# One kernel of a two-layer graph network: who makes two high parts, which bank one aggregate takes, and when its product follows

## The reference

```python
h = relu(layernorm(x))
x = x + L0(h, adj)          # two graph convolutions, then LSTMs over windows
h = relu(layernorm(x))
x = x + L1(h, adj)          # normalised adjacency, W1, batch norm, relu, W2, batch norm

def L0(x, adj):
    h = relu(adj @ (x @ Wg0 + bg0))
    h = relu(adj @ (h @ Wg1 + bg1))
    for p in 1, 2, 3, 4:    # windows of p tokens, an LSTM of p steps over each
        last = lstm_last(Wih[p-1], Whh[p-1], windows(h, p))
        h[:, p-1::p] = last # the last token of each window is replaced
    return h

def L1(f, A):
    A_norm = A + I
    A_hat = A_norm * dinv[:, None] * dinv[None, :]
    hid = relu(batchnorm((A_hat @ f) @ W1.T + b1))   # over batch and nodes
    return batchnorm(hid @ W2.T + b2)
```

## Time and profile before

| what | value |
|---|---|
| median of three runs | 531.46 us (528.65 to 533.92) |
| profiled execution, its own time | 531.53 us |
| its span in the trace | 529.6 us |
| PE busy | 506.1 us, 96% |
| DVE busy | 415.2 us, 78% |
| ACT busy | 345.1 us, 65% |
| POOL busy | 198.3 us, 37% |

### The profile page before, as it was taken

The page is one execution under the profiler, slowest core; times in us unless marked ns, Lnnn a source line. Parts: engine busy times, 40 slices in busy tenths (PEclk is TensorE's granted clock), DMA queues, the critical chain, the costliest instruction groups (busy, mean ns, idle before and its releaser), DMA issues.

```text
span 529.6 us, 8039 instructions
## 1 busy us (share of the span) xinstructions
PE 506.1 (96%) x2720; PEld 431.9 (82%) x2720; DVE 415.2 (78%) x954; ACT 345.1 (65%) x670; POOL 198.3 (37%) x307
## 2 busy tenths in 40 slices
PE   7999997999999999999999999999899999999994
PEld 5788776989987789999887899998678998875574
DVE  4688788878868888786689887875977887976875
ACT  3546866656777676675686675767657686448744
POOL 6403045131401854343007741511533423337940
PEclk9999999999999999999999999999989999999998
DMA  7403000000011112020210201012604000600008
GB/s 241 119 20 101 0 1 20 22 0 22 2 58 41 42 58 81 1 80 1 80 61 20 80 20 42 1 60 101 218 22 139 21 2 20 239 0 1 0 19 300
DMA packets 17597, 31.21 MB, mean 59 GB/s; under 512 B 1514, under 2 KB 6292, under 8 KB 17428
## 3 DMA queue, kind: packets, MB, share of 16 engines
q1 hardware_dynamic: 16564, 30.17, 16.8%
q10 hardware_dynamic: 992, 0.52, 0.4%
HBM read 19.16 MB, written 11.53 MB: 58 GB/s over the span
## 4 chain that ended last, share of the span: by engine, by line
PE 52%; issue 19%; DVE 10%; POOL 7%; ACT 6%; POOLq 3%; DVEq 1%; DMA 1%; ACTq 0%
PE gate_ps L1273 10%; PE gate_ps L1269 10%; PE gate_ps L1270 10%; PE pre_ps L1269 4%; PE pre_ps L1273 4%; PE pre_ps L1270 4%; POOL x_pre L447 3%; PE post_ps L1269 2%; POOLq L445 2%; PE post_ps L1270 2%; PE post_ps L1273 2%; DVE cell L1077 2%; ACT gate L764 2%; DVE cell L1102 1%; PE pre_ps L1337 1%
## 5 line engine op out<-in xcount | busy, mean ns | idle before, releaser
L764 ACT ACTIVATE gate<-gate_ps,gate_bias 128x256 f32<-128x256 f32 (+2 forms) x312 | 164.0, 563 | 41.3 <-PE gate_ps L1273 39.8
L1273 PE MATMUL gate_ps<-by_class_lo,wih_hi 128*128 128x256 f32 (+2 forms) x264 | 84.9, 322 | 4.2 <-POOL by_class_lo L477 4.2
L1269 PE MATMUL gate_ps<-by_class_hi,wih_hi 128*128 128x256 f32 (+2 forms) x264 | 85.4, 324 | 1.2 <-DVE by_class_hi L1058 1.0
L1270 PE MATMUL gate_ps<-by_class_hi,wih_lo 128*128 128x256 f32 (+2 forms) x264 | 84.2, 319 | 0.0
L774 ACT ACTIVATE gate<-cell 128x512 f32<-128x512 f32 (+2 forms) x88 | 45.4, 516 | 45.2 <-DVE cell L1077 24.3
L477 POOL TENSOR_TENSOR by_class_lo<-h,by_class_hi 128x256 fp32r<-128x256 f32 (+1 forms) x40 | 34.3, 858 | 82.1 <-ACT by_class_hi L772 82.1
L1273 PE MATMUL gate_ps<-hstep_lo,whh_hi 128*128 128x256 f32 (+2 forms) x192 | 61.5, 320 | 0.0
L1269 PE MATMUL gate_ps<-hstep_hi,whh_hi 128*128 128x256 f32 (+2 forms) x192 | 61.2, 319 | 0.2 <-DVE hstep_hi L1096 0.2
L1270 PE MATMUL gate_ps<-hstep_hi,whh_lo 128*128 128x256 f32 (+2 forms) x192 | 60.6, 315 | 0.0
L1273 PEld LDWEIGHTS gate_ps<-by_class_lo,wih_hi 128*128 128x128 f32 x264 | 50.3, 191 | 8.1 <-POOL by_class_lo L477 4.9
L1269 PEld LDWEIGHTS gate_ps<-by_class_hi,wih_hi 128*128 128x128 f32 x264 | 50.5, 191 | 6.0 <-DVE by_class_hi L1058 1.6
(11 more groups left out here) (320 smaller groups left out, 1295.0 us busy)
## 6 DMA issues: line engine op xcount, KB each, us to landing
x_pre<-in_x SPq DMA_DIRECT2D x16, 256.0 KB, 2.7
x<-in_x SPq DMA_DIRECT2D x16, 256.0 KB, 2.7
z_spill<-z_ring SPq DMA_DIRECT2D x8, 512.0 KB, 2.9
z_back<-z_spill SPq DMA_DIRECT2D x8, 512.0 KB, 5.6
x_spill<-x SPq DMA_DIRECT2D x12, 256.0 KB, 2.0
x_back<-x_spill SPq DMA_DIRECT2D x1, 3072.0 KB, 11.5
out<-x_back SPq DMA_DIRECT2D x11, 256.0 KB, 2.5
x<-in_adj SPq DMA_DIRECT2D x1, 1024.0 KB, 6.2
```

The lines of the kernel that those rows point to most:

```text
L764: nc.scalar.activation(gate[:, tile_of(g), gt, 0:size], gate_ps[k % GATE_BANKS][:, 0:size], ACT.Tanh if gt == G_GATE else ACT.Sigmoid, bia ...
L1269: nc.tensor.matmul(ps, w[0], m[0], start=start, stop=False)
L1270: nc.tensor.matmul(ps, w[1], m[0], start=False, stop=False)
L1273: return nc.tensor.matmul(ps, w[0], m[1], start=False, stop=stop)
```

## The change

Turns 68 and 69 are now in a list `ACT_HI`. For them ACT makes the high part, in the turn that follows, behind that turn's first gate and after h is done; DVE makes the low part at the start of its next turn. The transposes of batch 11 stand behind turn 70 instead of 69, into `post_ps` instead of `pre_ps`, and its `turned` is done within turn 71. Batch 7's aggregate takes `pre_ps` instead of `post_ps`, waits for `turned(9)` instead of `turned(10)`, and stands ahead of the transposes behind turn 70. Its first W1 half moves from behind turn 71 to behind turn 72, where the second stands. The two banks change places for every later aggregate and half up to batch 10.

```diff
+ACT_HI = [g for g in range(N_TURNS) if TURNS[g][0] == ROUNDS - 1 and TURNS[g][2] == 1 and TURNS[g][1] == CHAINS - 1]
...
-LAST_POS = {"agg": {CARRIED: 4, CARRIED + 1: 7, CARRIED + 2: 10, CARRIED + 3: 14},
-            "hid0": {CARRIED: 5, CARRIED + 1: 8, CARRIED + 2: 11, CARRIED + 3: 16},
+LAST_POS = {"turn": {BATCHES - PER_ROUND - 1: 4}, "agg": {CARRIED: 4, CARRIED + 1: 7, CARRIED + 2: 10, CARRIED + 3: 14},
+            "hid0": {CARRIED: 6, CARRIED + 1: 8, CARRIED + 2: 11, CARRIED + 3: 16},
...
-IN_NEXT_TURN = range(LAST_TURNED, LATE - 1)
+IN_NEXT_TURN = range(LAST_TURNED, LATE)
...
             unit = 3 * (n - CARRIED) + ("agg", "hid0", "hid1").index(kind)
-            return pre_ps if unit > 0 and unit % 2 else post_ps
+            return pre_ps if unit >= 0 and unit % 2 == 0 else post_ps
 
         def turn_ps(n):
 
-            return pre_ps if n >= LAST_TURNED and n % 2 else post_ps
+            return pre_ps if n == LAST_TURNED + 1 else post_ps
...
+                    if j == 0 and g - 1 in ACT_HI:
+                        q = TURNS[g - 1]
+                        act.wait_ge(h_done, g)
+                        hi = by_class[0][:, q[1], :].rearrange("h (t b) -> h t b", b=SUBS)[:, :, q[4]]
+                        nc.scalar.activation(hi, cell[:, tile_of(g - 1), :], ACT.Copy).then_inc(class_hi, 1)
...
+                if g - 1 in ACT_HI:
+                    q = TURNS[g - 1]
+                    hi, lo = (part[:, q[1], :].rearrange("h (t b) -> h t b", b=SUBS)[:, :, q[4]] for part in by_class)
+                    dve.wait_ge(class_hi, CLASS_AT[q[0], q[1], 1, q[4]])
+                    low(lo, cell[:, tile_of(g - 1), :], hi).then_inc(class_lo, 1)
                 if step > 0:
...
-                    nc.vector.tensor_copy(hi, c_).then_inc(class_hi, 1)
-                    if g not in POOL_LO:
+                    if g not in ACT_HI:
+                        nc.vector.tensor_copy(hi, c_).then_inc(class_hi, 1)
+                    if g not in POOL_LO and g not in ACT_HI:
...
+                if ("agg", CARRIED) in POST_AFTER[slot]:
+                    pe.wait_ge(x1_ready, LATE - 2)
+                    agg_mms(CARRIED, post_bank("agg", CARRIED), 1)
                 for kind, n in POST_AFTER[slot]:
...
+                        elif n == LATE - 1:
+                            pe.wait_ge(x1_ready, n)
...
-                    if kind == "agg":
-                        if n == CARRIED:
-                            pe.wait_ge(x1_ready, LATE - 1)
-                        elif n > CARRIED:
+                    if kind == "agg" and n != CARRIED:
+                        if n > CARRIED:
```

## The result

The changed kernel takes 526.77 us (median of seven runs, 526.21 to 527.95), the kernel before 531.19 us on the same chip. The ratio is 0.9933 with a 95% interval of 0.9908 to 0.9958: faster by 0.67%, or 2.2 to 4.9 us. The forecast was 527.8 with 525.8 to 530.8, and within 1%. On a second chip the ratio was 0.9948 (0.9928 to 0.9968).

What follows compares the result with a forecast made beforehand. DVE bounds turns 66 to 73 and TensorE follows. Terms 0.99 + 1.88 + 0.2 restarts + 1.6 clock - 1.0 new wait, 0.2 hand-overs, less 0.2 lateness, leave 3.7 us: 531.53 to 527.8, range 525.8 to 530.8.

Steps and rivals of the forecast that it cites:

- TensorE's order: Turns 70 to 73: new order and banks remove the 0.99 and 1.88 us pauses; turn 73 starts at 389.3, was 393.2.
- the whole 1.0: New TensorE wait in turn 72 on the step parts: 0.7 + 0.1 idle and some 0.15 of restart.
- DVE's chain: Turns 69 and 70: DVE loses two casts to ACT; cell products start at 376.2 (0.15 earlier) and 379.75 (was 380.30).
- the other end: Upper bound for ACT's copy of 512 elements to every second word, from L744's row: 1.14 us; lower bound 0.63.
- POOL's later copy: POOL's even copy of batch 15 waits for batch 11's transpose, now at 379.2; DVE asks at 383.9, so no cost.
- The part on ACT: Turns 68 and 69: ACT makes the high parts; DVE saves the cast (0.43), less ACT's 0.63 and its hand-over.
- the forecast's 0.55: Turn 70's cell product on DVE starts at 379.75 instead of 380.30; everything behind comes 0.55 to 0.6 earlier.
- The term of 1.6 us: TensorE's lower clock (0.66 in 385 to 390) after the 1.88 us pause no longer falls: 1.6 us gained.
- DVE's lateness at batch 8's W1 half: Batch 7's evictions and statistics behind turn 72 make DVE late for batch 8's low part: 0.2, bounds 0 and 0.68.
- (a): The clock still falls or ACT's copies are slow: 528.7 slow copies, 529.4 clock, 530.3 both; chance 0.20.
- (b): No change: DVE's queue at turns 72 and 73 gives the gain back at turns 73 to 75; 531, chance 0.10.
- (c): Slower: ACT stalls in turns 69 and 70 delay h; turn 70's step low part after 387.3; 533, chance 0.04.

Runs made afterwards that it cites:

- the nine copies by stride: Changed kernel with nine ACT copies of 128x512 added ahead of turn 0, writing every word, every second and every fourth, three each; no kernel time given.

## Why the prediction was right, and where it was not

**TensorE's order.** In the clock of before: turn 70 from 374.02 (374.03 forecast), the aggregate at 376.07 (376.1), the transposes at 378.79 (378.8), turn 71 at 379.15 (379.2). The 0.99 us pause is gone, and the 1.88 gave way to one of 0.62 in turn 72, with a shorter stop on the low part behind it. The forecast had 0.7 and 0.1 and called the whole 1.0; it is 1.16 (2.53 us for turn 72's first six matmuls, which take 1.37 in a full queue). This part is shown, by the profile and by the kernel with order and banks alone.

**DVE's chain.** Turn 69's cell product began at 376.20 (376.2), turn 70's at 379.70 (379.75). The copy took 0.675, 0.63 was taken, and 1.14 was the other end: the choice of the lower end was right. That both starts came out to 0.05 is luck in part, as two misses cancel. DVE's low part began 0.14 later than forecast each time (375.59 for 375.45, and 379.09 where the copy was to end at 378.95), from the longer copy and the hand-over behind it. And the cell product followed its start by 0.61 instead of 0.77, since the low part took 0.70 and 0.69. Before it took 0.84 and 0.85, both times beside a copy of the even tokens on POOL that had begun first; with POOL's copy held back the second takes 0.70. The rows of before for the second time:

```profile
378.49 0.93 POOL L488 COPY h<-cell 128x256 f32<-128x256 f32 x1 [2.42 <-DVE cell L1102]
```

```profile
378.93 0.85 DVE L884 TENSOR_TENSOR by_class_lo<-cell,by_class_hi 128x512 fp32r<-128x512 f32 x1
```

ACT's other two gates of turn 69 ended at 376.6 and not near 376.0, where the prediction's own numbers put them too (375.4 and two thirds of 1.83). It cost nothing: the cell product needs the first of them only, done at 376.04.

The step that failed is the sentence that POOL's later copy costs nothing. I looked at who waits for it, DVE at 383.9, and not at what it runs beside. With the move the low part became shorter by 0.16 and the cell product longer by 0.28, and turn 73 began at 389.6 instead of 389.3.

**Who earned it.** The part on ACT was worked out as if it brought turn 70's cell product forward: the cast gained, less the copy and its hand-over. The prediction never made the sum without it. Order and banks alone begin that product 13.09 us behind batch 8's first transpose (381.89 - 368.80), the changed kernel at 13.25. Before it is 380.30 - 366.45 = 13.85. So the forecast's 0.55 at this point was there with 0.60, but 0.76 was to be had without any ACT copy: 0.60 from `turned(11)` leaving (380.30 - 379.70 in the earlier trace rows), and 0.16 from the low part, which no longer has POOL's copy beside it.

**The clock.** The term of 1.6 us was in the sum with certainty, from one execution. It is 1.59 when it is there, and the second profile of before doesn't have it. At turn 73 the sum without it is 3.9 - 1.6 = 2.3, and 2.05 is what repeats; the missing 0.25 is about the 0.28 by which the cell product became longer. The measured 4.4 us between the medians, 3.6 by the ratio, have more in them than this: the clock also falls behind round 0's pause, which the change doesn't touch, in some runs and not in others. So that the ratio gives the forecast's 3.7 almost to the tenth is luck in part: 2.0 of it is shown, and the rest isn't. The lowest group of clocks, 0.986 to 0.990, has 19 of the 57 runs of before and none of the 18 of the changed kernel. That fits a fall behind the removed pause, but it doesn't show one, since order and banks alone, which lack that pause too, have two of twelve runs there. No experiment settled how much of the difference between the medians is the clock behind the removed pause and how much is the draw of the runs.

**Given back later.** I took off 0.2 for DVE's lateness at batch 8's W1 half. From turn 73 to that half is 9.76 us in both profiles of before, 10.20 and 10.12 in the changed kernel: 0.4, twice what I took off, inside the bounds of 0 and 0.68. It doesn't last: from batch 8's transposes to batch 12's it is 82.15 in the second profile of before and 80.18 in the changed kernel, 1.97 less, against 2.05 at turn 73.

**The rivals.** (a) had slow copies and a falling clock: neither came. (b) would have the gain gone by turn 75: the 1.97 says no. (c) asked for the step low part after 387.3; it was there at 383.7 in the clock of before (382.15 + 0.69 + 0.84). With each copy made twice the kernel is still not slower than before.

## What to carry to other kernels

When a change has two parts, make the sum for each alone: here one part carried all of the fixed gain and the other cost 0.44 us of it, and the total hid this. An instruction that moves in time costs by what it now runs beside, even if nobody waits for it. A lower clock seen once in a profile is a term with a chance, not a term; a distance between two instructions at equal clock told apart 0.1 us where medians of a dozen runs could not tell 1 us.

## What the runs showed of the hardware

The clock after a pause isn't decided by the pause's length alone. The same 1.88 to 1.89 us pause of TensorE was followed by 0.66 over 5 us in one execution of the kernel before and by 1.00 in another. The pause of 2.38 to 2.40 us in round 0 was followed by 0.50 in both profiles of before, in the second of the changed kernel and in six others, and by 1.00 in the first of the changed kernel, with ACT copies only, with the copies made twice, and with the nine copies by stride. Behind a pause of 1.43 us (ACT copies only) and behind all shorter ones in turns 70 to 73 it was 1.00, and behind the one of 4.03 us it was 0.50.

ACT's copy of 512 words took 0.62 us to every word, 0.66 to every second and 1.10 to 1.12 to every fourth. The Trainium skill, "SBUF — State Buffer", section "Door 1: The DMA port swizzle", asks for two hits on a 16-byte line; the step between the second and the third agrees.

Which of DVE and POOL pays more for the two running at once went with who began first, in these profiles. In the changed kernel POOL's copy began 0.17 us ahead of the cell product: 0.76 and 0.96 us, where they take 0.65 and 0.69 apart from each other. With order and banks alone it began 0.03 us behind it (381.92 against 381.89), and the cell product took 0.68 while POOL's copy took 1.19:

```profile
381.92 1.19 POOL L489 COPY h<-cell 128x256 f32<-128x256 f32 x1 [3.50 <-PE post_ps L1377]
```

The one behind wasn't held until the other was done: in the changed kernel POOL's copy ended at 379.45, and the cell product, over at 379.82, has only 0.37 us behind that, where it takes 0.69 alone.
